# Decoder layer on one core: x and context transposed by DMA per batch, with a new order of steps and new PSUM banks

## The reference, cut to what matters

```python
# x, ctx: (16, 128, 256) float32; 16 heads of 16; 8 experts, 2 chosen per token
x = layernorm(x + attn(x))          # q = softmax over d, k = softmax over tokens, state = k^T v,
                                    # out = layernorm(q state) @ Wo.T + bo
x = layernorm(x + xattn(x, ctx))    # 16-head softmax attention of x on ctx
x = layernorm(x + ffn(x))           # top-2 of 8 experts, gelu
```

## Time and profile before

| | us |
|---|---|
| median of 3 runs | 491.59 |
| lowest, highest | 488.96, 493.59 |
| the profiled execution: its time | 483.46 |
| its span | 481.4 |
| PE busy | 373.9 (78%) |
| DVE busy | 293.9 (61%) |
| POOL busy | 248.1 (52%) |
| ACT busy | 223.0 (46%) |
| mean granted TensorE clock | 0.896 of full |

### The profile page before, as it was taken

One profiled execution on the slowest core, in us unless ns is written; L12 is line 12 of the kernel. 1 busy time (PEld: TensorE's weight loads), 2 busy tenths in 40 slices (PEclk: granted clock), 3 DMA queues, 4 the chain that ended last, 5 costly groups with the idle time before them and its releaser, 6 DMA issues.

```text
span 481.4 us, 12128 instructions
## 1 busy us (share of the span) xinstructions
PE 373.9 (78%) x4065; PEld 298.8 (62%) x4065; DVE 293.9 (61%) x759; ACT 223.0 (46%) x528; POOL 248.1 (52%) x309
## 2 busy tenths in 40 slices
PE   3585999999999999999875381997797988999200
PEld 1454777777777777777653360785585766788100
DVE  2558789888888888888667910444242444444162
ACT  2241676666666666667654000534341344444014
POOL 7243456667665665676520075174655546644362
PEclk9797999999999999999997557799799889999855
DMA  7230222443223333332332032353547536543394
GB/s 236 60 126 12 67 68 67 123 122 106 65 83 117 122 121 124 99 99 83 130 100 66 0 89 87 59 148 80 111 110 132 105 83 121 117 103 89 99 328 141
DMA packets 53483, 50.54 MB, mean 105 GB/s; under 512 B 26417, under 2 KB 47538, under 8 KB 53426
## 3 DMA queue, kind: packets, MB, share of 16 engines
q1 hardware_dynamic: 46834, 35.61, 27.6%
q0 software_dynamic: 4416, 12.06, 8.2%
q10 hardware_dynamic: 2176, 2.10, 1.3%
HBM read 25.64 MB, written 18.61 MB: 92 GB/s over the span
## 4 chain that ended last, share of the span: by engine, by line
PE 66%; issue 10%; DVE 7%; ACT 6%; another core or an unknown queue 5%; DMA 3%; POOL 2%; ACTq 0%; DVEq 0%; SPq 0%; POOLq 0%
PE bank L319 25%; PE bank L1463 12%; PE bank L1125 10%; PE bank L1130 4%; PE bank L1355 3%; PE bank L1340 3%; PE bank L1359 3%; PE bank L1240 2%; ACT rows_all L643 2%; PE bank L1255 2%; PE bank L1257 1%; DMA EW<-parts 1%; ACT rows_all L718 1%; PE bank L1336 1%
## 5 line engine op out<-in xcount | busy, mean ns | idle before, releaser
L526 POOL DMA_INDIRECT parts<-QKT,home x46 | 48.2, 1047 | 67.1 <-DVE QKT L1053 57.1
L1045 DVE TENSOR_TENSOR R<-scratch,QV 128x512 f16<-128x512 f32 x46 | 31.8, 692 | 71.0 <-ACT scratch L695 49.4
L695 ACT ACTIVATE scratch<-bank 128x512 f32<-128x512 f32 x46 | 27.7, 603 | 86.6 <-remote 45.4
L449 POOL TENSOR_TENSOR rstd<-veps,neghalf 128x1 f32<-128x1 f32 x48 | 38.5, 802 | 42.6 <-DVE veps L779 42.4
L1463 PE MATMUL bank<-EW,QV 128*128 x368 | 57.8, 280 | 2.5 <-DVE R L1045 1.3
L1463 PEld LDWEIGHTS bank<-EW,QV 128*128 128x128 f16 x368 | 36.8, 101 | 8.8 <-issue 3.7
L319 PE MATMUL bank<-V,EW 128*128 128x256 f16 x264 | 35.9, 289 | 7.5 <-issue 7.4
L916 DVE TENSOR_REDUCE NM<-bank 128x4 bf16<-128x512 f32 x64 | 39.5, 680 | 1.6 <-PE bank L1306 1.6
L456 POOL TENSOR_SCALAR X<-R,mv,rstd 128x256 f32<-128x256 f32 x30 | 37.0, 1234 | 5.3 <-POOL rstd L449 5.3
L517 POOL DMA_INDIRECT TX<-x2d,home x24 | 24.4, 1018 | 28.8 <-DVE home L1020 21.8
L643 ACT ACTIVATE rows_all<-bank 128x512 f32<-128x512 f32 x64 | 33.0, 603 | 10.4 <-PE bank L1340 10.4
(11 more groups left out here) (224 smaller groups left out, 936.8 us busy)
## 6 DMA issues: line engine op xcount, KB each, us to landing
x2d<-blank SPq DMA_DIRECT2D x16, 384.0 KB
scratch<-w_in SPq DMA_DIRECT2D x8, 512.0 KB, 3.9
scratch<-w_out SPq DMA_DIRECT2D x8, 512.0 KB, 3.9
x2d<-X SPq DMA_DIRECT2D x32, 128.0 KB, 4.2
XC<-x SPq DMA_DIRECT2D x16, 128.0 KB, 3.6
XC<-ctx SPq DMA_DIRECT2D x16, 128.0 KB, 3.3
EW<-parts SPq DMA_DIRECT2D x8, 256.0 KB, 7.0
EW<-parts ACTq DMA_DIRECT2D x8, 256.0 KB, 7.7
```

The costliest lines, as they stand in the source:

```text
L449: pool.tensor_tensor(rstd[n][p][:], veps[n][p][:], neghalf[:, 0:1], ALU.pow).then_inc(s_rs[n], 1)
L526: pool.indirect_dma_start(parts, bass.IndirectOffsetOnAxis(ap=home[:, HALVES * t + f:HALVES * t + f + 1], axis=0), Y[t % 2][:, f, :], None ...
L695: act.activation(dst[t % 2][:, 2 * g:2 * g + 2, :], chunks(bank[2 * (t % 2) + g], 2, TW), ACT.Gelu, scale=2.0 / WSCALE).then_inc(signal, 1)
L1045: dve.tensor_tensor(HL[t % 2][:, part, :], HF[t % 2][:, part, :], HH[t % 2][:, part, :], ALU.subtract)\
```

## The change

For batches 2 to 15 the input is no longer transposed by PE. ACT copies `XC` itself, untransposed, as float16 into one buffer `XCS` (step `xh`), POOL subtracts (step `xl`), and one DMA transpose of 128x1024 float16, issued by SP (step `turn`), writes `XCT`, of which `XCTh` and `XCTl` are now the halves. DVE's `XCTl` is gone except for batches 0 and 1, which keep PE's transposes ahead of the loop and at the first `qv`. SP loads batch b + 1 in iteration b. Every engine has another order, several steps have another lag (`kk` 1, `st`, `oT`, `ao` and `kv2` 2, `x1T`, `q2` and `nat` 3, `mT` and `sc` 4, `x2T` 5 on PE; `xb` and `qs` 1, `x1b` 3 on POOL), the steps use other PSUM banks, and the `through` waits, which guard those banks, follow. Two small tiles of the second half now lie in `X2T`.

```diff
-        XCTh = pair("XCTh", [P, 2 * KC, P], f16)
-        XCTl = pair("XCTl", [P, 2 * KC, P], f16)
+        XCS = sb("XCS", [P, 2, 2 * KC * P], f16)
+        XCT = pair("XCT", [P, 2, 2 * KC, P], f16)
+        XCTh, XCTl = ([t[:, v, :, :] for t in XCT] for v in range(2))
...
-        B_XC, B_QV, B_KK, B_QK, B_ST, B_O, B_S0, B_AO, B_X1, B_KV = 4, 0, 7, 0, 1, 3, 4, 6, 3, 2
-        B_Q2, B_Q2B, B_MT, B_PV, B_AO2, B_X2, B_GH, B_BO2, B_FOLD = 5, 0, 5, 7, 1, 0, 6, 5, 6
-        NAT_BANK, SC_BANK = (0, 7, 6, 5), (2, 1, 4, 3)
+        B_XC, B_QV, B_KK, B_QK, B_ST, B_O, B_S0, B_AO, B_X1, B_KV = 3, 5, 2, 2, 4, 4, 5, 6, 3, 1
+        B_Q2, B_Q2B, B_MT, B_PV, B_AO2, B_X2, B_GH, B_BO2, B_FOLD = 3, 0, 0, 7, 5, 1, 6, 0, 6
+        NAT_BANK, SC_BANK = (5, 0, 4, 3), (0, 2, 6, 7)
...
             def emit(step, b, p, half):
-                if step == "load" and past(b, 2):
-                    sp.wait_ge(s_xcT, b - 1)
-                    sp.wait_ge(s_xb, b - 1)
-                    load(half, p)
+                if step == "load" and 1 <= b < NB - 1:
+                    if b < 3:
+                        sp.wait_ge(s_xcT, b)
+                    else:
+                        sp.wait_ge(s_xl, b - 2)
+                    sp.wait_ge(s_xb, b)
+                    load((b + 1) // 2, 1 - p)
+                if step == "turn" and b >= 2:
+                    sp.wait_ge(s_xl, b - 1)
+                    sp.wait_ge(s_qv_ps, b - 1)
+                    sp.wait_ge(s_k_ps, b - 1)
+                    sp.wait_ge(s_kv_ps, b - 1)
+                    sp.dma_start_transpose(XCT[p][:].rearrange("p v k t -> p (v k) t"),
+                                           XCS[:].rearrange("p v n -> p (v n)")).then_inc(s_xct[p], 16)
...
-            pipeline("load/0 weights/0 keep/7", emit)
+            pipeline("load/0 keep/7 turn/0 weights/0", emit)
...
+                if step == "xl" and b >= 2:
+                    pool.wait_ge(s_xcTh, b + 1)
+                    pool.tensor_tensor(XCS[:, 1, :], XC[p][:].rearrange("p k d -> p (k d)"), XCS[:, 0, :], ALU.subtract)\
+                        .then_inc(s_xl, 1)
...
-            pipeline("pw0/2 qn/1 n1/2 xb/0 x1b/2 n2/5 nr/4 qs/0", emit)
+            pipeline("xl/0 qs/1 xb/1 n2/5 pw0/2 qn/1 x1b/3 n1/2 nr/4", emit)
...
+                if step == "xh" and b >= 2:
+                    act.wait_ge(s_xld[p], 8 * b + 16 - 8 * p)
+                    act.wait_ge(s_cld[p], 8 * b + 16 - 8 * p)
+                    if b >= 3:
+                        act.wait_ge(s_xct[1 - p], 16 * ((b - 1) // 2))
+                    copy(XCS[:, 0, :], XC[p][:].rearrange("p k d -> p (k d)"), s_xcTh)
...
-            pipeline("ex0/4 ex1/4 ex2/4 ex3/4 XCTh/0 qkT/1 X2T/6 K2/2 X1T/2 MTc/3 V2/2 lns/4 rec/4 ewh/0 "
-                          "gcp/6 OT/1 qe/0 ke/0 QM0/2", emit)
+            pipeline("MTc/4 xh/0 X2T/6 X1T/3 ex0/4 ex1/4 qe/1 ex2/4 K2/2 OT/2 QM0/3 ex3/4 ke/1 ewh/0 V2/2 "
+                          "lns/4 rec/4 qkT/1 gcp/6", emit)
...
-                if step == "XCTl":
-                    dve.wait_ge(s_xcTh, b + 1)
-                    dve.tensor_tensor(XCTl[p][:], chunks(bank[B_XC], 2 * KC), XCTh[p][:], ALU.subtract).then_inc(s_xcTl, 1)
...
-            pipeline("mx0/3 mx1/3 mx2/3 mx3/3 XCTl/0 R2/5 s2/5 ewl/1 STm/1 O2T/4 qvsb/0 qmax/0 s0/1 kmax/0 "
-                          "QM1/2 R1/1 qsum/0 s1/1 krec/0", emit)
+            pipeline("qsum/1 s0/2 QM1/3 kmax/1 R1/2 mx0/3 s1/2 mx1/3 mx2/3 mx3/3 O2T/4 krec/1 qvsb/0 ewl/1 "
+                          "qmax/0 STm/1 R2/4 s2/4", emit)
...
+            def turn_input(b):
+                pe.wait_ge(s_xld[b], 16)
+                pe.wait_ge(s_cld[b], 16)
+                if b == 1:
+                    pe.wait_ge(s_xcTl, 1)
+                turn(bank[B_XC], lambda c: XC[b][:, c, :], 2 * KC).then_inc(s_xcT, 1)
+
+            def input_turned(b, p):
+
+                if b < 2:
+                    pe.wait_ge(s_xcTl, b + 1)
+                else:
+                    pe.wait_ge(s_xct[p], 16 * (b // 2))
...
-            pipeline("xcT/0 qk/1 ao2/5 x1T/2 x2T/6 pv/4 mT/3 st/1 qv/0 gh/6 oT/1 kk/0 q2/2 ao/1 sc/3 nat/2 "
-                         "kv2/1", emit)
+            pipeline("mT/4 st/2 x1T/3 sc/4 ao2/5 kv2/2 oT/2 q2/3 kk/1 ao/2 nat/3 pv/4 qk/1 qv/0 gh/6 x2T/5", emit)
```

More of the change, by code:

```diff
@@ L263, in decoder_layer @@
         s_cld = [sem(f"s_cld{p}") for p in range(2)]
+        s_xl = sem("s_xl")
+        s_xct = [sem(f"s_xct{p}") for p in range(2)]
         s_xcT, s_xcTh, s_xcTl, s_xb = sem("s_xcT"), sem("s_xcTh"), sem("s_xcTl"), sem("s_xb")
@@ L572, in emit @@
             def emit(step, b, p, half):
-                if step == "XCTh":
+                if step == "xh" and b < 2:
                     act.wait_ge(s_xcT, b + 1)
[L575 to L580, removed]
-                        weights_high(1)
-                        weights_high(2)
+                    copy(XCTh[p], chunks(bank[B_XC], 2 * KC), s_xcTh)
+                    if b == 0:
+                        weights_high(1)
+                if step == "xh" and b >= 2:
[4 more added lines that the diff above has]
+                    copy(XCS[:, 0, :], XC[p][:].rearrange("p k d -> p (k d)"), s_xcTh)
                 if step == "ke":
@@ L737, in weights_low, with low_of @@
                                              ALU.mult, ALU.subtract).then_inc(s_wsp_l, 1)
+            def low_of(b):
+                dve.wait_ge(s_xcTh, b + 1)
+                dve.tensor_tensor(XCTl[b], chunks(bank[B_XC], 2 * KC), XCTh[b], ALU.subtract).then_inc(s_xcTl, 1)
             weights_low(0)
+            low_of(0)
+            weights_low(1)
             def fold():
@@ L856, in emit @@
                                       ALU.max).then_inc(s_qmax, 1)
+                    if first:
+                        low_of(1)
                 if step == "qsum":
@@ L867, in emit @@
                     dve.reciprocal(krec[p][:], ksum[p][:]).then_inc(s_krec, 1)
+                    if first:
+                        weights_low(2)
                 if step == "STm":
@@ L1166, in rows32 @@
                 return slice(32 * u, 32 * u + 32)
+            pe.wait_ge(s_cstb, 1)
+            turn_input(0)
             def emit(step, b, p, half):
@@ L1170, in emit @@
                 first = counted and b == 0
[L1172 to L1181, removed]
                 if step == "qv":
@@ L1184, in emit @@
                         pe.wait_ge(s_wsp_l, KC)
-                    pe.wait_ge(s_xcTl, b + 1)
-                    through(s_x2sb, 1, 1, b - 6)
+                    input_turned(b, p)
+                    through(s_mx, 4, 1, b - 3)
                     if counted:
-                        through(s_mx, 4, 1, b - 3)
-                        through(s_qkT, 1, 1, b - 1)
-                        through(s_qm1, 2, 2, b - 3)
+                        through(s_bs[0], 1, 1, b - 2)
                         through(s_qv_sb, 1, 1, b - 1)
+                        through(s_r2, 1, 1, b - 5)
                     token_major(bank[B_QV][:, :], CQV, 2 * D, XCTh[p], XCTl[p]).then_inc(s_qv_ps, 1)
+                    if first:
+                        turn_input(1)
                 if step == "kk":
@@ L1212, in emit @@
                 if step == "kv2":
+                    input_turned(b, p)
                     if first:
                         pe.wait_ge(s_wsp_l, 3 * KC)
-                    through(s_ex, 4, 1, b - 2)
+                    through(s_x2sb, 1, 1, b - 4)
                     if counted:
@@ L1234, in emit @@
                     pe.wait_ge(s_qkT, b + 1)
-                    through(s_r2, 1, 1, b - 4)
+                    through(s_mx, 4, 3, b - 2)
                     if counted:
-                        through(s_ex, 4, 2, b - 3)
+                        through(s_oT, 1, 1, b - 1)
                         through(s_st, 2, 2, b - 1)
@@ L1263, in emit @@
                     pe.wait_ge(s_oT, b + 1)
-                    through(s_gcp, 1, 1, b - 5)
+                    through(s_ex, 4, 3, b - 2)
                     if counted:
-                        through(s_mx, 4, 3, b - 2)
+                        through(s_gcp, 1, 1, b - 5)
                         through(s_r1, 1, 1, b - 1)
@@ L1270, in emit @@
                     pe.wait_ge(s_x1, b + 1)
-                    through(s_ex, 4, 4, b - 2)
+                    through(s_mx, 4, 4, b - 1)
                     if counted:
-                        through(s_oT, 1, 1, b)
+                        through(s_qm0, 2, 2, b - 1)
                         through(s_x1sb, 1, 1, b - 1)
```

85 lines of the change are left out of this document (38 added, 47 removed).

## The result

The changed kernel takes 530.34 us (median of 4 runs, 523.95 to 534.67), the kernel before 490.27 (4 runs) on the same chip. The ratio is 1.086, with a 95% interval from 1.073 to 1.099. Executions of one kernel fall into quicker and slower ones, and every ratio here is taken from the quicker ones of both kernels, so that it can differ a little from the ratio of the medians. The profiled execution took 532.83 us, its span is 531.0. The forecast of 504.0 had the right sign, and the time lies above its range of 489 to 516.

What follows compares the result with a forecast made beforehand. PE bounds the kernel before; POOL, waiting for stores, was to bound iterations 7 to 14. The terms -0.9 + 14.2 - 0.9 = +12.4 us, added to the 491.6 median, gave 504.0 us, range 489 to 516.

Steps and rivals of the forecast that it cites:

- the wait and its cause: On POOL before `n2`, iterations 7 to 14: stores of `keep`, issued behind `load` and `xb`, cost a 5.6 us wait.
- the transpose by DMA is hidden: On SP: the transposed tile is there at 8.3 us after `xb`, before `qv` needs it; otherwise 5.2 us would show.
- PE's time can be had: On PE: the `XC` transposes and the wait before `kv2` go, 1.02 us an iteration, from 13.72 to 12.70.
- With the wait POOL's own round is 9.87 + 5.6 = 15.5 us, and it becomes the bound.: On POOL, iterations 7 to 14: work plus the store wait sets the round, 8 x (15.5 - 13.72) = +14.2 us.
- The port: On DVE and POOL: a shared port pair could delay POOL at `xl` by up to 1.22 us, forecast 10 us later.
- The tie of the two chains: On SP's dependents: POOL's round with the store wait, 15.5 us, ties with the chain through the weights, 15.7; 15.5 was kept.
- the second chain: From `xb` through SP's `turn` and `weights`, ACT's `ewh`, then `O2T` and `nr`, to the next `xb`: 15.7 us a round.
- Batches 5 and 6: The two rounds after `qv` of batch 4: 12.4 us each instead of 12.83, together -0.9 us.
- ahead of batch 4: From the start to `qv` of batch 4: both lists level, 0 us, with 5 us either way.
- batch 15: Iteration 15, without `load`: SP runs ahead again, 12.8 - 13.72 = -0.9 us.
- The drain: After `qv` of batch 15: short chains of latency with the same steps, 0 us, with 3 either way.
- The clock: On PE, with 2.8 us idle an iteration: the first 2.8 us a lower clock would cost are paid from that.

Runs made afterwards that it cites:

- e1: The changed kernel with SP issuing the stores of `keep` before `load`: ratio 1.052 to the kernel before, rounds of 14.68 us.
- e11: The changed kernel with its SP order kept, but `load` bringing the batch of its own iteration: ratio 1.023 to the kernel before, rounds of 13.86 us.
- e7: The changed kernel with DVE's `ewl` moved ahead of `R1`: ratio 1.067 to the kernel before, rounds of 16.85 us.
- e10: e9 with DVE's `ewl` also moved ahead of `R1`: 489.16 against 487.04 us for the kernel before, ratio 1.014, rounds of 13.57 us.
- e2: The changed kernel with `weights` first on SP, `keep` still behind `load`: ratio 1.087 to the kernel before, rounds of 17.85 us.
- e9: The changed kernel with SP's order keep, weights, load, turn: 485.12 against 487.04 us for the kernel before, ratio 1.003, rounds of 13.12 us.
- e6: The changed kernel with the zeros for the spare rows issued after the two stores of `X2`: ratio 1.067 to the kernel before, rounds of 16.59 us.
- e4: The kernel before, with `keep` also waiting for `xb` of the same iteration: 448.78 against 445.69 us, ratio 1.006.

## Why the prediction was right in kind and too small

**Right: the wait and its cause.** `keep` behind `load` behind `xb` of the same iteration, `n2` waiting for it in eight rounds, 5.4 us against 5.6, is shown by the rows of after, by e1, which takes `keep` out from behind, and by e11, which takes the event away. The parts are near too. Over the eight rounds the loads take 0.86 us (0.9 forecast), the issue of `keep` 1.0 in six of them and 1.9 and 1.6 in two (1.02), and from the last store's issue to POOL's next start it is 2.7 to 4.5 us, 3.2 in the mean (3.6). The Trainium skill (DMA: Bandwidth & Descriptors, "Anatomy of one DMA — SWDGE (gpsimd) path") gave an estimate of 2.3 us for that store. Its fit is for DMAs that POOL issues, and these are SP's; no round here is as quick (the eight landings take 2.6 to 4.4 us), and the mean wait is 1.1 us above the 4.3 that followed from it.

**Right: the transpose by DMA is hidden. Right in part: PE's time can be had.** PE waits for the transpose once in the run, 1.5 us ahead of 33.9, and in none of the eight rounds. With SP's order mended the round is 13.12, where I took 12.70 for the floor: 0.60 of the 1.02 us. PE's busy time fell by 0.23 us a round and not by 0.44, its idle time from 0.58 to 0.21.

**The step that failed: "With the wait POOL's own round is 9.87 + 5.6 = 15.5 us, and it becomes the bound."** The round is 17.43 us. I took POOL's round as work plus one wait, as if its other inputs were always there. The profile gives for a round: busy 79.19 / 8 = 9.90, the store 5.38, `veps` 0.99, `NT` 0.71, its own powers 0.35. That is 17.33 of the 17.43. Against my sum the multiply of `nr` is 0.99 longer beside `ewl`, `xl` is 0.29 shorter (1.16), the store 0.2 shorter, and the waits for DVE are 1.6 us above the 0.09 that the sum had; what is left, -0.1, is instructions that overlap. So of the two us that a round is longer, the largest term is the wait for DVE, put at nearly nothing, and the next is the multiply. The waits are no accident: `pw0` stands behind `n2`, DVE's `R1` waits for it 35.2 us in eight rounds, and POOL's `n1` then waits for `R1`'s statistics. A late POOL makes DVE late, and that makes POOL late. In the old order these waits lay inside PE's round.

**The port.** The multiply at 1.72 us beside L965 (1.22 us) and at 0.73 without it, in e7 and e10, agrees with the rule of the Trainium skill cited in the prediction (SBUF — State Buffer, "SBUF: two separate sides"). The 0.99 us that it costs is a little less than the 1.15 for which `ewl` still runs when the multiply starts. I had priced the rule for `xl`, which did not meet `ewl` in these rounds, and not for `nr`. e7 measures what it costs where POOL sets the round: 0.58 us, 5 in all.

**The tie of the two chains.** I counted the second chain (weights, `ewh`, `V2`, `lns`, `rec`, `O2T`, `nr`) at 15.7 and kept the other. It is there, and by itself it makes a round of 14.68 (e1). The first alone, with the weights in time, makes 17.85 with a wait of 6.1 us (e2), which would be about 17.1 with the 5.4 us of the changed kernel. So the second adds little while the first is there, and the two did not tie: the first was well above my 15.5, the second below my 15.7.

**Batches 5 and 6, -0.9 forecast, +3.4 measured.** I gave them PE's gain and forgot that `weights` stands behind the load there too. In these two rounds `ewh` waits 1.9 and 1.6 us, and e2 with the weights in front takes all of it away (25.77 against 29.10). The same holds for 2.2 of the 2.7 us ahead of batch 4. So the second chain was worked out for eight rounds only, though its cause begins with the first load in the loop. In batch 15, -0.9 forecast and +0.4 measured, SP's order has 0.9 of the difference: e9 takes 13.17 there.

**The drain, 0 forecast, +4.3 measured.** The same steps with longer lags are not free at the end, as e9 shows, whose gain of 4.7 us at the last `qv` is gone at the second half. The 3 us either way were too narrow. What in it does this stays open.

**A slip in the prediction's sums.** By its own formula a round of 14.6 us gives 496.8 and not 499; 499 belongs to a round of 14.9. The range of 489 to 516 does not hang on it.

**The clock.** I wrote that the first 2.8 us of a lower clock would be paid from PE's idle time. The granted clock of the eight rounds is 0.91, and `qv` takes about 2.7 us instead of 1.46 in six of them. In e9, e11 and e1, where PE idles for 0.2 to 1.5 us a round, it is 1.00, and here PE idles for 2.9; but in e6 PE idles for 3.2 us a round and the clock is 1.00. So idle time a round does not tell the clock by itself. Nor is the lower clock why the round is above 15.5: e6 takes 16.59 at full clock with a wait of 4.0, where my sum would give 9.87 + 4.0 = 13.9. What the clock costs can be estimated. From one `xb` to the next, less the wait for the store in between, the eight rounds take 11.76, 12.09, 11.78, 12.62, 11.93, 11.77, 11.77 and 12.69 us. The first and the sixth ran at full clock, four others are within 0.35 of them, and the two long ones are 0.9 above. By that a slower PE is about 2.2 us of the 29.7, an estimate, and the sentence held nearly.

## What to carry to other kernels

When a queue engine's step gets a newer event to wait for, everything behind it in that queue inherits the event; go through the whole queue for each of them and for each stage of the loop, from its first iteration. In a loop of engines that wait for each other, a new wait can bring further waits with it, so add up the waits of the engine's round in the order of its list, not its work and one wait. Put what others wait for (`keep`, `weights`) ahead of what waits (`load`), and count the drain whenever lags grow.

## What the runs showed of the hardware

**The second half differs between chips, with the same instructions.** It takes 225 us in the profiled execution of before and 187 in e4's, which runs the same second half on another chip. Much of the difference lies in waits that no instruction of this core explains. The list for before, from 256.3 us on:

```profile
ACT scratch L695 <- remote: 45.4, 6, 9.8
PEld bank L319 <- issue: 30.1, 26, 11.5
ACT QS L570 <- issue: 19.1, 1, 19.1
```

The same stretch of e4 has no `remote` line at all, and this for the second:

```profile
PEld bank L319 <- issue: 3.9, 2, 2.0
```

All ratios are therefore taken within a session, and the times of the first half compared by the evictions.

**An issue on SP has no fixed price.** The first DMA of `keep` occupied SP for 0.43 us in the earlier trace rows and in six of the eight rounds of the changed kernel, and for 1.32 and 1.00 in the other two. The 1.32 is in the rows of SP of the section on the result.
